# Attention on one core of a Trainium2: another place for the sums over V in TensorE's queue

## The reference

```python
qkv = (h @ w_qkv + b_qkv).reshape(B, N, 3, nh, hd).transpose(2, 0, 3, 1, 4)
q, k, v = (qkv[0], qkv[1], qkv[2])
attn = jax.nn.softmax(jnp.einsum('bhqd,bhkd->bhqk', q, k) * hd ** (-0.5), axis=-1)
o = jnp.einsum('bhqk,bhkd->bhqd', attn, v).transpose(0, 2, 1, 3).reshape(B, N, C)
```

## Time and profile before

| | |
|---|---|
| median of 3 executions | 1630.94 us (1626.31 to 1634.62) |
| the profiled execution | 1625.62 us |
| its span, first to last instruction | 1623.9 us |
| mean granted clock of TensorE | 0.922 of 2.4 GHz |
| TensorE busy | 1400.8 us (86%) |
| VectorE busy | 1092.9 us (67%) |
| ScalarE busy | 798.2 us (49%) |
| GpSimd busy | 647.2 us (40%) |

### The profile page before, as it was taken

One profiled execution on the slowest core, in us unless ns is written; L12 is line 12 of the kernel. 1 busy time (PEld: TensorE's weight loads), 2 busy tenths in 40 slices (PEclk: granted clock), 3 DMA queues, 4 the chain that ended last, 5 costly groups with the idle time before them and its releaser, 6 DMA issues. The chain is left out here.

```text
span 1623.9 us, 25041 instructions
## 1 busy us (share of the span) xinstructions
PE 1400.8 (86%) x8657; PEld 870.6 (54%) x8657; DVE 1092.9 (67%) x1859; ACT 798.2 (49%) x1537; POOL 647.2 (40%) x873
## 2 busy tenths in 40 slices
PE   4787988998899879987789899999977299999995
PEld 2563333333333458976633333333325299999995
DVE  3657878887797254446489889889926556656663
ACT  0441766766677552225327677677763233333331
POOL 0125767767720000001269999995004612112121
PEclk9995989998899989998859999999998599999998
DMA  7275577657720309003660222220019466767673
GB/s 187 63 201 99 137 190 166 179 174 174 178 90 3 136 10 292 1 1 95 187 103 11 47 46 46 46 47 3 3 61 356 145 204 189 238 189 236 187 234 77
DMA packets 93396, 204.22 MB, mean 126 GB/s; under 512 B 35846, under 2 KB 61384, under 8 KB 90028
## 3 DMA queue, kind: packets, MB, share of 16 engines
q1 hardware_dynamic: 59788, 121.26, 23.4%
q0 software_dynamic: 33488, 81.41, 22.5%
HBM read 131.56 MB, written 72.12 MB: 125 GB/s over the span
## 5 line engine op out<-in xcount | busy, mean ns | idle before, releaser
L958 DVE TENSOR_REDUCE att_neg_max<-att_for_max 128x1 f32<-128x1024 f32 x512 | 601.7, 1220 | 106.5 <-PE att_for_max L1033 103.8
L943 ACT ACTIVATE att_probs<-att_scores 128x512 f32<-128x512 f32 x1002 | 523.9, 606 | 262.3 <-PE att_scores L1072 261.8
L1083 PE MATMUL att_out<-att_probs,V 128*32 128x512 f32 x2048 | 283.9, 627 | 3.9 <-ACT att_probs L943 2.0
L1072 PE MATMUL att_scores<-att_QS,att_KS 56*128 56x512 f32 x618 | 235.1, 467 | 38.1 <-DMA att_QS<-att_neg_max_rows 21.2
L1033 PE MATMUL att_for_max<-att_KS,att_QS 54*128 54x512 f32 x640 | 247.8, 474 | 0.7 <-DVE att_neg_max L958 0.5
L1072 PEld LDWEIGHTS att_scores<-att_QS,att_KS 56*128 56x128 f32 x618 | 105.4, 192 | 205.1 <-ACT att_probs L943 140.9
L1033 PE MATMUL att_for_max<-KS,QS 54*128 54x512 f32 x384 | 165.9, 535 | 25.8 <-DVE att_neg_max L958 13.1
L1875 ACT ACTIVATE experts_gelu<-experts_proj,experts_b 128x256 f32<-128x256 f32 x171 | 81.3, 475 | 208.6 <-PE experts_proj L1944 185.4
L1944 PE MATMUL experts_proj<-experts_x_parts,w_parts 128*128 128x256 f32 (+1 forms) x1197 | 174.1, 286 | 1.4 <-DVE experts_x_parts L1669 1.4
L1823 POOL DMA_INDIRECT sums_of_experts<-experts_y,experts_rows x38 | 61.3, 1613 | 260.0 <-DVE experts_y L1705 254.2
L1072 PE MATMUL att_scores<-QS,KS 56*128 56x512 f32 x384 | 150.7, 466 | 12.2 <-ACT att_probs L943 10.7
(11 more groups left out here) (227 smaller groups left out, 2004.9 us busy)
## 6 DMA issues: line engine op xcount, KB each, us to landing
w_parts<-w_parts SPq DMA_DIRECT2D x20, 2304.0 KB, 8.7
w_parts<-att_w_parts POOLq DMA_DIRECT2D x15, 864.0 KB, 5.9
w_parts<-w_parts SPq DMA_DIRECT2D x5, 2592.0 KB, 15.6
qk_halves<-qkv_qk_parts SPq DMA_DIRECT2D x40, 288.0 KB
w_parts<-att_w_parts POOLq DMA_DIRECT2D x20, 576.0 KB, 5.6
slot_rows<-mlp_blank_rows SPq DMA_DIRECT2D x2, 5145.0 KB, 28.2
att_QS<-qk_halves POOLq DMA_DIRECT2D x120, 72.0 KB
att_KS<-qk_halves POOLq DMA_DIRECT2D x60, 144.0 KB
```

The source lines that it names most:

```text
L943: nc.scalar.activation(PR[st % 2][:, j, :], score_bank(st, n), ACT.Exp, scale=SCALE).then_inc(exp_done, 1)
L958: nc.vector.tensor_reduce(negm[half][:, c:c + 1], psM[ring % 2][:].rearrange("p a n -> p (a n)"), AX_X, ALU.max, negate=True).then_inc(rin ...
L1072: nc.tensor.matmul(score_bank(st, n), KS[g % SLOTS][rows, p, k * P:(k + 1) * P], QS[g % SLOTS][rows, half, p, :], start=True, stop=True).t ...
L1083: last = nc.tensor.matmul(psO[32 * j:32 * j + 32, :], T.V[:, g, k, 32 * j:32 * j + 32], PR[st % 2][:, j, :], start=(k == 0), stop=(k == KT ...
```

## The change

In the loop of TensorE's queue the call of `weigh(st - 1)` moves from behind the last half of the step to between its second and third score (behind the half that follows the second score). Nothing else is changed: the waits of each instruction are the same, and so are the queues of the other engines.

```diff
@@ -1101,14 +1101,14 @@
                 score(st, 1)
                 if units:
                     max_half(units[0], 1)
+                if st:
+                    weigh(st - 1)
                 score(st, 2)
                 if units:
                     max_half(units[1], 0)
                 score(st, 3)
                 if units:
                     max_half(units[1], 1)
-                if st:
-                    weigh(st - 1)
                 if (span := span_turned(st)) is not None:
                     turn(span)
                 if (span := span_behind(st, SPREAD_LAG)) is not None:
```

## The result

| | before | after |
|---|---|---|
| median | 1632.48 us (1626.31 to 1634.62, 4 runs) | 1704.66 us (1701.97 to 1711.75, 4 runs) |
| the profiled execution | 1625.62 us | 1711.75 us |
| mean granted clock | 0.922 | 0.904 |

The ratio is 1.0469, 95% interval 1.0433 to 1.0506: slower, 72 us in the medians, 86 between the two profiled executions (the one after is the longest of its four). The forecast was 1699. Medians are over all executions of a kernel; a ratio leaves out those more than 1.5% above its shortest one.

A forecast was written before the change was run, and what follows sets the result against it. The prediction took a loop of waits, not an engine's work, to bound the kernel. Longer steps added 86.6 us, shorter DMA stalls gave back 15: net +71.6, 1697 against the profiled execution, forecast 1699, range 1672 to 1726.

The forecast's parts named there:

- W: A step's run of sums over V on TensorE; forecast to wait for the fourth exponential of the step before.
- E4: The fourth exponential of a step on ScalarE; forecast to be what the moved sums and the third score need.
- S3: The third score of a step on TensorE; forecast to stand behind the moved sums, starting 1.00 us after them.
- E3: The third exponential of a step on ScalarE; forecast 0.59 us behind its score, with ScalarE's idle now before it.
- E1: The first exponential of a step on ScalarE; on the old loop, 0.59 us behind its score, forecast to leave it.
- The copy: Span's first sums wait for ScalarE's copy of the bank they overwrite: +0.97 us, net 0.91 for 14 steps, 12.7 a layer.
- Transpose and spread: Steps transposing maxima or spreading inverses lose the sums' cover of a reduction wait: +0.91 us each; net 9.9 and 6.4 a layer.
- M1: A step's first half for the maxima on TensorE; behind a transpose or spread, forecast to wait openly for the second reduction.
- R2: A step's second reduction on VectorE; forecast to end at 3.66 us, its wait no longer hidden by the sums.
- rival (C): Slower still: the clock falls to half at each of 28 copies for one step, 36 us more, 1735 us; 14%.
- (A): Faster: in ordinary steps later scores are served while the sums wait; VectorE bounds a step at 2.41 us, 1565 total; 4%.
- (B): Level: DMA stalls swallow the longer steps, reduction and copy waits hidden; 1637 us; 4% within 0.5%, 3% just above.

The follow-up runs named there:

- the exchange of waits: The kernel of before with ScalarE's two waits ahead of each step's first exponential in the other order; 1623.75 us, ratio 0.9987.
- the run with the doubled scores: The changed kernel with the first and second score of each of a layer's last eleven steps issued twice; 1681.71 us, ratio 1.0354 to before.

## Why the prediction was right

**The loop.** W stands on E4, W, S3, E3, E4, as worked out; an ordinary step was put at 2.73 us and is 2.67. The term that failed is the 0.59 from score to exponential, read at E1 and used for E3, which stands at 0.54; the exchange of waits showed why. 7.0 us a layer forecast, 0 measured.

**The copy.** 0.97 forecast for the wait, 0.96 in the trace, the step 3.65: 0.98 over an ordinary one and 0.92 over before's excess, 12.9 us a layer for 12.7. The idle of 0.97 in one row of before was the right model for it.

**Transpose and spread.** The wait of M1 for R2 is bare, as said. The steps are 1.06 and 1.07 over an ordinary one where 0.91 was forecast: 0.06 of it because the ordinary step is 2.67, 0.09 because W follows M2 at 0.32 and not at 0.23, the spacing of two halves. And the reciprocals' time on VectorE, which I had counted as hidden, adds 0.11 to the step before. With the excess of before taken off: 0.86 x 14 + 0.65 x 13 + 0.11 x 14 = 22.0 us a layer for 16.3.

**The last eleven steps** were the largest miss in size. Forecast was the new loop at full clock, 7.3 us a layer. ScalarE's timeline of the changed kernel, where the first one's third exponential is E1 of step 117, and the last exponentials of the stage:

```profile
541.19 2.07 ACT L943 ACTIVATE att_probs<-att_scores 128x512 f32<-128x512 f32 x4 [0.60 <-PE att_scores L1072]
...
580.38 0.59 ACT L943 ACTIVATE att_probs<-att_for_max 128x512 f32<-128x512 f32 x1
```

From 542.16 (541.19 + 0.97) to 580.97 are 38.8 us, for 23.8 before: 15.0, and the second stage is within 0.3 of it. The loop at full clock is 6.8 of this by the run with the doubled scores, which is the 7.3 of the forecast; the other 8.2 is the clock at 0.50, a term that the sum did not have. That was rival (C), with 14%, and with another place: I put its price on the copy steps with maxima around them, where the clock held, and not on the last steps, where TensorE has no maxima to compute and idles 1.92 for the copy instead of 0.97. At full clock even that long idle cost no more than forecast: 3.64 for the step instead of 2.67, in the run with the doubled scores.

**The sum.** 12.9 + 22.0 + 15.0 = 49.9 a layer, 99.8 for two, against 82.2 in the windows; so by difference the stalls on DMAs gave back 17 or 18, where I had taken 15. What TensorE's matmuls waited for these DMAs fell by about as much, from 31.2 us to 11.2 (their weight loads' waits fell by 38); the largest group, before and after (us, times, longest):

```profile
PE att_scores L1072 <- DMA att_QS<-att_neg_max_rows: 21.2, 8, 4.3
PE att_scores L1072 <- DMA att_QS<-att_neg_max_rows: 8.5, 5, 2.9
```

The terms that were too high (ordinary step, 7.0 us a layer for 0) and too low (transpose and spread by 5.7, last steps by 7.7) came to 86.6 together where 99.8 was right. That the number fits all the same is partly luck. Forecast were 71.6 us more; the medians differ by 72.2, the profiled executions, from which the terms come, by 86.1, and the execution profiled after happened to be the longest of its four. The range was too narrow at its lower end as well: it took 16 us for waits for R2 that are hidden after all, which is 9.9 + 6.4 for one layer, and two layers have 33.

Put back one at a time the three kinds of step gave 35, 41 and 36 us, more in sum than the whole. Two reasons are in the traces: the clock's part in the last steps comes back with two of them (28 us of last steps with W back there, 12 with W back at the copy), and the stalls stay short in each (7.7 to 18.2 us of matmuls' waits for 11.2 with the change whole and 31.2 before), so what they gave back is not taken away again. The cost of crossing between the places works the other way.

**The rivals.** (A), S3 served while W waits, did not happen: S3 stands 0.99 to 1.00 behind the W shown, and ordinary steps were no shorter. (B) failed as the copy and R2 were not hidden, though the stalls gave back some 18 us.

## What to carry to other kernels

When a run of instructions is moved within a queue that nothing else bounds, look for the loop that it leaves and for the one that it joins, and then for what it hid where it stood: here the ordinary step stayed at 2.67 us, and the 72 us came from waits that it had covered (a reduction, a copy) and from the steps at the end, where it had been free. Cost each kind of step by itself, the rare ones first. In a stretch where TensorE already waits the clock can go as well, and a wait then costs more than itself: here the fall took some 8 us a layer besides the 7 of the loop. And if a block is put back in some steps only, price the crossing: here 0.72 us around the transpose and the spread, nothing around the copy.

## What the runs showed of the hardware

- Less work made it slower: with sums over half of the columns the granted clock went to 0.69 and 0.60 over the attention stages and the median from 1705 to 1777 us. With 44 more matmuls in the last steps it went from 1705 to 1682, and the clock there from 0.50 to 0.86 and 1.00.
- Of two waits ahead of one instruction, the order in the program decides what the late one costs: 0.59 or 0.53 us from a score to its exponential, on ScalarE; 0.06 us in an ordinary step, 0.31 in a span of eight.
- A stall on DMAs moves with the place where it is waited for: with a step more of lead, two long steps of 5.44 and 8.38 us became one of 7.27, and the next span began 0.8 us earlier.
